# Attention phase: feed-forward products through one PSUM bank, the double banks for scores alone

## The chip, the cores and the metric

The kernel runs on one core of one Trainium2 chip. Its time is device microseconds from start to end of the program. The profile's busy times, waits and orders come from one profiled execution. TensorE does matmuls and transposes into PSUM (eight banks of 512 fp32 columns a partition), ScalarE exponentials and other functions, VectorE and GpSimd elementwise work, SyncE issues DMAs. The engines run side by side, each in its own order, and wait for each other by semaphores.

## The reference

Two layers; the change is in the attention phase of the first. It computes causal attention of 8 heads with two maps each over 4 x 1024 tokens of 128 channels, and, independent of it, the feed-forward gate of the same tokens, with its inputs rounded blockwise to a 4-bit grid:

```python
scores = jnp.einsum('bhqd,bhkd->bhqk', q, k)
scores = jnp.where(causal[None, None], scores, -jnp.inf)
attn = jax.nn.softmax(scores.astype(jnp.float32), axis=-1).astype(scores.dtype)
...
out = jnp.einsum('bhqk,bhkd->bhqd', attn, v)
...
gate = fp4_linear(x, w_gate)     # rounds x and w in blocks of 16, then a product
y = fp4_linear(x, w_up)
h = jax.nn.silu(gate) * y
return fp4_linear(h, w_down)     # rounds h too
```

## The kernel before

`attention_phase` works in `ITER` = 8 iterations: the first and the last written out, six in a loop on every engine. An iteration handles two slots (a slot is four score maps, each of 8 head dimensions in a row group of 32) and four feed-forward tiles of 128 tokens (`GT` = 4).

A slot is ten units (`NU`), listed by `chunk_units`: a unit is 512 columns of queries against one block of 128 keys. Blocks on the diagonal have fewer columns; units 1 and 8 join 384 and 128 columns ("in two pieces"), units 2 and 9 have 256 columns ("narrow"). For each unit TensorE makes scores in two pairs of maps (`scores`, L933): a pair fills a double bank of a ring of three (`ring`), one bank for each of its maps. ScalarE turns a pair into probabilities (`exp`, L787). GpSimd masks diagonal blocks (`mask`, L731). Three units later TensorE multiplies by the values into `ps_o` (`values`, L953). VectorE turns `ps_o` (L839) and divides.

A feed-forward tile goes: gate product (`gate`, L961), ScalarE's tanh (L801), VectorE's first product (L846), up product (`up`, L965), VectorE's second product (L851), seven steps that round the hidden rows (`fp4_part`), three transposes (`turn_hidden`, L972), VectorE's copies (L861, L862), down product (`down`, L978), tanh (L806), VectorE's product (L865). Once an iteration x is rounded for the next in seven such steps (`round_x`), turned (`turn_x`, L918) and copied (L843).

No scheduler sets the order. Each engine's `place(it, n)` is called for ticks n = 0 to 79 (four a unit), and for what is left of the iteration before at n + 80; in it each piece of work stands at a fixed tick. What an engine issues is the order of those calls, and semaphores alone set the time. The ring is dealt out by a list of its uses in order:

```python
GATE, HIDDEN, DOWN, CHUNK = 3, 7, 9, 11
ORDER = [("x", 0)]
for k in range(STEPS):
    if k % PERIOD == GATE:
        ORDER.append(("gate", k // PERIOD))
    ORDER += [("scores", k, 0), ("scores", k, 1)]
```

So 45 uses an iteration: 40 for scores, four for gate and up products, which share a double bank until VectorE's second product, and one for the turned x. `wait_free` makes TensorE wait until the third use before is finished. `ps_f`, a single bank, holds the turned hidden rows and the down product.

## Time and profile before

| what | value |
| --- | --- |
| three runs | 751.53, 753.23, 757.88 us; median 753.23 |
| the profiled execution | 757.34 us, of which the span is 755.6 |
| busy in the span: TensorE | 609.4 us (81%) |
| VectorE | 531.1 us (70%) |
| ScalarE | 497.5 us (66%) |
| GpSimd | 323.8 us (43%) |
| ScalarE's exponentials (L787) | 320, 280.1 us busy |
| values (L953) | 1536 matmuls, 158.3 us busy |
| scores (L933) | 672 matmuls in the loop and after, 80.1 us busy |

The span runs from the first to the last instruction. The attention phase is the stretch from 115.2 us to about 454 us. An engine's busy time counts the time in which at least one of its instructions runs; instructions that follow each other on ScalarE, VectorE and TensorE overlap by a part of their duration, so starts tell more than durations. A row of the order of time reads: start, duration, engine, line, output and input, number of instructions merged, and in brackets how long the engine was idle before and whose result ended that.

### The profile page before, as it was taken

To read this page: it belongs to the slowest core of one execution; us is meant where nothing else is said; L and a number is where in the kernel's file an instruction comes from. 1 tells how busy PE (TensorE), PEld (TensorE's weight loads), DVE (VectorE), ACT (ScalarE), POOL (GpSimd) and SP (SyncE) were. 2 spreads that over 40 slices of the span, in tenths; PEclk is the share of its full clock that TensorE was granted. 3 is DMA by queue.
4 is the path that set the end of the run, shared out by engine and by line. 5 is a ranking of instruction groups with operands and counts; after the bars stand their busy time and mean duration, and the time that the engine had idled before them with its cause. 6 is when DMAs were issued, how large, how long until landed. Compare 5 with 4: busy or idle time off the path is not lost. (4 is left out here: it accounts for less than half of the span.)

```text
span 755.6 us, 15892 instructions
## 1 busy us (share of the span) xinstructions
PE 609.4 (81%) x4825; PEld 365.0 (48%) x4826; DVE 531.1 (70%) x1428; ACT 497.5 (66%) x843; POOL 323.8 (43%) x463
## 2 busy tenths in 40 slices
PE   4567666999999999999999997866873787888970
PEld 3455451333333333333333346655762686777860
DVE  3999996879798888888897777964734342434475
ACT  2277875989898999989898971432423454656561
POOL 0243354444343444344444435154645355554551
PEclk9899996999999999999999998996977799999995
DMA  7000001004555555666566005111112122222285
GB/s 198 15 28 23 19 1 56 1 2 87 97 91 97 85 87 89 105 105 105 105 105 106 3 1 196 35 38 55 55 50 57 47 75 64 65 79 66 77 244 149
DMA packets 76264, 56.05 MB, mean 74 GB/s; under 512 B 6528, under 2 KB 70848, under 8 KB 75968
## 3 DMA queue, kind: packets, MB, share of 16 engines
q1 hardware_dynamic: 70688, 46.01, 29.1%
q0 software_dynamic: 4352, 8.99, 3.5%
q10 hardware_dynamic: 1184, 0.56, 0.3%
q8 instruction: 20, 0.33, 0.2%
q14 instruction: 20, 0.16, 0.1%
HBM read 15.36 MB, written 28.65 MB: 58 GB/s over the span
## 5 line engine op out<-in xcount | busy, mean ns | idle before, releaser
L787 ACT ACTIVATE attend_prob<-attend_ring 128x1024 f32<-128x1024 f32 (+1 forms) x320 | 280.1, 951 | 17.5 <-PE attend_ring L933 15.5
L731 POOL TENSOR_SCALAR_AFFINE_SELECT attend_prob<-attend_prob 128x256 f32<-128x256 f32 x256 | 118.6, 488 | 142.4 <-ACT attend_prob L787 141.1
L953 PE MATMUL attend_ps_o<-attend_prob,attend_v_slot 128*32 128x512 f32 (+3 forms) x1536 | 158.3, 501 | 0.0
L1906 POOL DMA_INDIRECT expert_outputs<-routed_linear_gated,routed_expert_goal_now x72 | 70.9, 985 | 69.3 <-DVE routed_linear_gated L1950 55.0
L1033 POOL DMA_INDIRECT slots<-rows,slot_index x64 | 61.7, 964 | 67.5 <-issue 37.2
L933 PE MATMUL attend_ring<-attend_qk_slot 32*128 32x512 f16 (+3 forms) x672 | 80.1, 329 | 8.1 <-ACT attend_prob L787 6.3
L933 PEld LDWEIGHTS attend_ring<-attend_qk_slot 32*128 32x128 f16 x672 | 22.4, 91 | 106.7 <-ACT attend_prob L787 37.6
L1927 DVE TENSOR_TENSOR outed_linear_head_normed<-outed_linear_head_normed,routed_linear_ps_c 128x256 f32<-128x256 f32 x72 | 30.2, 420 | 50.1 <-ACT outed_linear_head_normed L2020 31.0
L2067 PE MATMUL routed_linear_ps_c<-outed_linear_head_normed,head_turned 128*128 128x128 f32 x384 | 54.5, 288 | 6.1 <-ACT outed_linear_head_normed L1996 5.0
L2020 ACT ACTIVATE outed_linear_head_normed<-routed_linear_ps_c 128x256 f32<-128x256 f32 x72 | 27.5, 382 | 47.2 <-PE routed_linear_ps_c L2067 36.1
L953 PEld LDWEIGHTS attend_ps_o<-attend_prob,attend_v_slot 128*32 128x32 f32 x1536 | 33.9, 109 | 45.8 <-issue 38.3
L2067 PEld LDWEIGHTS routed_linear_ps_c<-outed_linear_head_normed,head_turned 128*128 128x128 f32 x384 | 49.7, 202 | 7.0 <-ACT outed_linear_head_normed L1996 4.6
L369 POOL TENSOR_TENSOR project_parts_q<-project_rotated_q,project_parts_q 128x1024 f16<-128x1024 f32 x8 | 17.6, 2202 | 68.8 <-ACT project_parts_q L417 68.8
L839 DVE STREAM_TRANSPOSE attend_o_t<-attend_ps_o 128x512 f32<-128x512 f32 x32 | 22.9, 717 | 18.3 <-PE attend_ps_o L953 18.3
L2001 ACT ACTIVATE head_turned<-w 128x512 f32 x48 | 30.4, 634 | 4.4 <-issue 4.4
L1542 ACT ACTIVATE routed_linear_qk_square<-routed_linear_ps_c 128x512 f32<-128x512 f32 x16 | 9.5, 592 | 36.1 <-PE routed_linear_ps_c L1650 19.9
L1650 PE MATMUL routed_linear_ps_c<-att_w,routed_linear_xn_turned 128*128 128x384 f32 x64 | 29.2, 588 | 4.7 <-DVE routed_linear_qk L1248 4.7
L978 PEld LDWEIGHTS attend_ps_f<-down_w,attend_hq_t 128*128 128x128 f32 (+1 forms) x192 | 23.8, 190 | 17.8 <-issue 16.4
L2076 PE MATMUL routed_linear_ps_f<-w,outed_linear_head_normed 128*128 x144 | 24.2, 292 | 9.7 <-DVE outed_linear_head_normed L1927 5.6
L978 PE MATMUL attend_ps_f<-down_w,attend_hq_t 128*128 128x128 f32 (+1 forms) x192 | 29.9, 292 | 1.1 <-DVE attend_hq_t L862 1.1
L394 ACT ACTIVATE qk_parts<-project_ps_turn 128x1024 f16 (+1 forms) x30 | 29.0, 1021 | 2.6 <-PE project_ps_turn L475 2.6
L2076 PE MATMUL routed_linear_ps_b<-w,outed_linear_head_normed 128*128 x144 | 24.1, 292 | 7.3 <-DVE routed_linear_gated L1950 5.8
(290 smaller groups left out, 1285.7 us busy)
## 6 DMA issues: line engine op xcount, KB each, us to landing
slots<-attend_zeros SPq DMA_DIRECT2D x24, 715.0 KB, 10.3
attend_qk_slot<-qk_parts SPq DMA_DIRECT2D x14, 512.0 KB, 3.1
x_pairs<-slots SPq DMA_DIRECT2D x72, 65.0 KB
v_all<-expert_outputs SPq DMA_DIRECT2D x8, 512.0 KB
xn_all<-project_xn SPq DMA_DIRECT2D x8, 256.0 KB, 2.3
w<-w_laid SPq DMA_DIRECT2D x1, 2048.0 KB, 7.8
rows<-rows SPq DMA_DIRECT2D x4, 512.0 KB
out<-xn_all SPq DMA_DIRECT2D x8, 256.0 KB, 3.7
```

The costliest lines, as they stand in the source:

```text
L731: ins = nc.gpsimd.affine_select(out=edge, in_=edge, compare_op=ALU.is_ge, fill=0.0, base=0, pattern=[[0, 2], [1, P]], channel_multiplier=-1)
L787: nc.scalar.activation(probs(k, pair)[:, :, 0:width], scores[:, :, 0:width], ACT.Exp, scale=HD ** -0.5).then_inc(exp_made[u][pair], 1)
L933: ins = nc.tensor.matmul(dst[:, s * QC + at:s * QC + at + cols], qk[rows, T + j * P:T + (j + 1) * P], qk[rows, qc * QC + off:(qc + 1) * QC ...
L953: ins = nc.tensor.matmul(ps_o[RB * s:RB * (s + 1), off:QC], v4[slot][:, j, s], probs(k, s // 2)[:, s % 2, at:at + cols], start=j == 0, sto ...
L978: ins = nc.tensor.matmul(ps_f[:, 0:P], hq_t[0:r, c * P:(c + 1) * P], m.down_w[0:r, c * P:(c + 1) * P], start=c == 0, stop=c == 2)
L1033: pool.indirect_dma_start(m.slots, bass.IndirectOffsetOnAxis(m.slot_index[u][c][:, j:j + 1], 0), m.rows[c][:, t * ROW:(t + 1) * ROW], None ...
L1650: ins = nc.tensor.matmul(bank_pair(part)[:, j, 0:3 * C], xt[:, tile * P:(tile + 1) * P], m.att_w[:, 4 * P:7 * P], start=True, stop=True)
L1906: pool.indirect_dma_start(m.outputs, bass.IndirectOffsetOnAxis(goal_now[i][:, j:j + 1], 0), y_out[i][:, j * P:(j + 1) * P], None).then_inc ...
L1927: nc.vector.tensor_tensor(act_e[c], silu[c], ps_h[c][:, EI:2 * EI], ALU.mult).then_inc(a_made, 1)
L2001: nc.scalar.activation(w_now[s % 3], m.w13[:, ds(expert * (2 * EI), 2 * EI)], ACT.Copy).then_inc(w_kept, 1)
L2067: ins = nc.tensor.matmul(ps_h[s % 3][:, f * P:(f + 1) * P], w_now[s % 3][:, f * P:(f + 1) * P], x_t[s % 3], start=True, stop=True)
L2076: ins = nc.tensor.matmul(ps_y[s % 2][:, 0:P], act_e[s % 3][:, c * P:(c + 1) * P], m.w2[:, ds(expert * EI + c * P, P)], start=c == 0, stop= ...
```

## The change

Seven things, all in `attention_phase`:

- Gate and up products, the turned x, the turned hidden rows and the down product all go through `ps_f`, one after the other. The gate product waits until an earlier tile's down product is read, the up product until VectorE's first product has read the gate (`u_made`), the hidden transposes until its second has read the up product (`h_made`).
- The ring is used by scores alone, 36 times an iteration.
- A narrow unit's two pairs share one double bank, side by side in its columns. [...] One exponential of 1024 columns takes the place of two of 512, one mask of four blocks the place of two.
- The unit before a narrow one issues its first pair at its own step and its second at the narrow unit's.
- Tiles start at ticks 0, 20, 40 and 60 (in the first iteration at 12, 28, 44 and 60). Counted from a tile's start, the gate product stands at tick 1, up at 5, the transposes of the tile before at 9 and its down product at 13. x is turned at tick 77.
- VectorE's steps stand at other ticks; x's rounding is at 18, 19, 38, 39, 58, 58 and 59.
- The end of the last iteration follows these places.

The core of the diff:

```diff
-        GATE, HIDDEN, DOWN, CHUNK = 3, 7, 9, 11
-        PERIOD = STEPS // GT
-        ORDER = [("x", 0)]
+        GATE, UP, HIDDEN, DOWN = 1, 5, 9, 13
+        FIRST_TURN, NEXT_TURN, CHUNK = 9, TICKS - 3, 46
+        ORDER = []
         for k in range(STEPS):
-            if k % PERIOD == GATE:
-                ORDER.append(("gate", k // PERIOD))
-            ORDER += [("scores", k, 0), ("scores", k, 1)]
+            ORDER += [("scores", k, pair) for pair in range(1 if k % NU in NARROW else 2)]
...
+                if u in NARROW:
+                    nc.scalar.activation(prob[2 * k % PROBS], buffer("scores", k, 0), ACT.Exp, scale=HD ** -0.5).then_inc(exp_made[u][0], 1)
+                    return
...
+                for part, tick in enumerate((18, 19, 38, 39, 58, 58, 59)):
...
-                wait_free(it, "scores", k, pair)
-                dst = buffer("scores", k, pair)
+                if u in NARROW and pair == 1:
+                    pe.wait_ge(first_pair_made[u], 2 * it + slot + 1)
+                else:
+                    wait_free(it, "scores", k, pair)
+                dst = buffer("scores", k, 0 if u in NARROW else pair)
                 for j, off, at, cols in segs:
+                    at += pair * HALF if u in NARROW else 0
...
             def gate(it, i):
                 pe.wait_ge(xt_kept, it + 1)
-                wait_free(it, "gate", i)
-                nc.tensor.matmul(buffer("gate", i)[:, 0:INNER], xq_t[:, i * P:(i + 1) * P], m.gu_w[:, 0:INNER], start=True,
+                if i == 1 and isinstance(it, int) and it == 0:
+                    pe.wait_ge(h_made, 1)
+                elif i >= 1:
+                    pe.wait_ge(g_made, 4 * it + i - 1)
+                nc.tensor.matmul(ps_f[:, 0:INNER], xq_t[:, i * P:(i + 1) * P], m.gu_w[:, 0:INNER], start=True,
                                  stop=True).then_inc(gate_made, 1)
 
             def up(it, i):
-                nc.tensor.matmul(buffer("gate", i)[:, QC:QC + INNER], xq_t[:, i * P:(i + 1) * P], m.gu_w[:, INNER:2 * INNER],
+                pe.wait_ge(u_made, 4 * it + i + 1)
+                nc.tensor.matmul(ps_f[:, 0:INNER], xq_t[:, i * P:(i + 1) * P], m.gu_w[:, INNER:2 * INNER],
                                  start=True, stop=True).then_inc(up_made, 1)
 
             def turn_hidden(it, i):
                 pe.wait_ge(hq_made, 4 * it + i + 1)
-                once(pe, g_made, 4 * it + i)
+                if isinstance(it, int) and it == ITER - 1 and i == GT - 1:
+                    pe.wait_ge(g_made, 4 * it + i)
+                else:
+                    pe.wait_ge(h_made, 4 * it + i + 2)
...
             def place(it, n):
                 k, tick = divmod(n, 4)
...
+                if k < STEPS and tick == 0:
+                    if k % NU in NARROW:
+                        scores(it, k - 1, 1)
+                    scores(it, k, 0)
+                    if (k + 1) % NU not in NARROW:
+                        scores(it, k, 1)
...
+                if n == NEXT_TURN and not (isinstance(it, int) and it == ITER - 1):
+                    turn_x(it + 1)
+                if (i := at_tile(it, n, GATE)) is not None:
+                    gate(it, i)
+                if (i := at_tile(it, n, UP)) is not None:
+                    up(it, i)
+                if (i := behind_tile(it, n, HIDDEN)) is not None:
+                    turn_hidden(it, i)
+                if (i := behind_tile(it, n, DOWN)) is not None:
+                    down(it, i)
                 if tick == 2 and 0 <= k - LAG < STEPS:
                     values(it, k - LAG)
```

TensorE in the loop, around the first slot's second tile, before (L972 transposes, L961 gate, L965 up, L933 scores, L953 values):

```order
L953 MATMUL attend_ps_o<-attend_prob,attend_v_slot 32x512 x4
L972 MATMUL attend_ps_f<-ident,attend_hq 128x128 x2
L972 MATMUL attend_ps_f<-ident,attend_hq 96x128
L961 MATMUL attend_ring<-gate_up_w,attend_xq_t 128x352
L933 MATMUL attend_ring<-attend_qk_slot 128x384 x2
L933 MATMUL attend_ring<-attend_qk_slot 128x128 x2
L965 MATMUL attend_ring<-gate_up_w,attend_xq_t 128x352
L933 MATMUL attend_ring<-attend_qk_slot 128x384 x2
L933 MATMUL attend_ring<-attend_qk_slot 128x128 x2
L953 MATMUL attend_ps_o<-attend_prob,attend_v_slot 32x512 x4
```

And now (L996 gate, L1001 up, L1011 transposes, L962 scores, L985 values):

```order
L962 MATMUL attend_ring<-attend_qk_slot 128x512 x4
L996 MATMUL attend_ps_f<-gate_up_w,attend_xq_t 128x352
L985 MATMUL attend_ps_o<-attend_prob,attend_v_slot 32x256 x4
L962 MATMUL attend_ring<-attend_qk_slot 128x512 x4
L1000 REGISTER_ALU
L1001 MATMUL attend_ps_f<-gate_up_w,attend_xq_t 128x352
L985 MATMUL attend_ps_o<-attend_prob,attend_v_slot 32x512 x4
L962 MATMUL attend_ring<-attend_qk_slot 128x512 x4
L1011 MATMUL attend_ps_f<-ident,attend_hq 128x128 x2
L1011 MATMUL attend_ps_f<-ident,attend_hq 96x128
L985 MATMUL attend_ps_o<-attend_prob,attend_v_slot 32x512 x4
```

The gate product stands alone between scores and values, one step before the up product, the transposes of the tile before come a step later, and no pair of scores stands behind the up product.

TensorE in the loop, at units 1 and 2 of the first slot, before:

```order
L933 MATMUL attend_ring<-attend_qk_slot 128x384 x2
L933 MATMUL attend_ring<-attend_qk_slot 128x128 x2
L86 ISA
L933 MATMUL attend_ring<-attend_qk_slot 128x384 x2
L933 MATMUL attend_ring<-attend_qk_slot 128x128 x2
L953 MATMUL attend_ps_o<-attend_prob,attend_v_slot 32x384 x4
L953 MATMUL attend_ps_o<-attend_prob,attend_v_slot 32x128 x4
L933 MATMUL attend_ring<-attend_qk_slot 128x256 x4
L953 MATMUL attend_ps_o<-attend_prob,attend_v_slot 32x256 x4
```

And now:

```order
L1001 MATMUL attend_ps_f<-gate_up_w,attend_xq_t 128x352
L985 MATMUL attend_ps_o<-attend_prob,attend_v_slot 32x384 x4
L985 MATMUL attend_ps_o<-attend_prob,attend_v_slot 32x128 x4
L86 ISA
L962 MATMUL attend_ring<-attend_qk_slot 128x384 x2
L962 MATMUL attend_ring<-attend_qk_slot 128x128 x2
L962 MATMUL attend_ring<-attend_qk_slot 128x256 x4
L1005 ISA
L1009 REGISTER_ALU
L1011 MATMUL attend_ps_f<-ident,attend_hq 128x128 x2
L1011 MATMUL attend_ps_f<-ident,attend_hq 96x128
L985 MATMUL attend_ps_o<-attend_prob,attend_v_slot 32x256 x4
```

Unit 1's second pair has moved behind the values of one step, next to unit 2's four matmuls of 256 columns; the up product and the transposes stand in the gaps.

VectorE in the loop, between the third tile's rounding and the fourth tile's products, before (L573, L576 of `attend_xq`: x's steps; L882: the sum of head squares; L846, L851: the two products):

```order
L821 TENSOR_TENSOR attend_o_scaled<-attend_o_t,attend_rden 128x256
L573 SCALAR_TENSOR_TENSOR attend_xq_power<-attend_xq 128x512
L576 SCALAR_TENSOR_TENSOR attend_xq<-attend_xq_power,attend_xq 128x512
L882 ISA
L882 TENSOR_REDUCE head_var<-attend_head_square 128x32
L839 STREAM_TRANSPOSE attend_o_t<-attend_ps_o 128x512
L861 COPY attend_hq_t<-attend_ps_f 128x256
L862 COPY attend_hq_t<-attend_ps_f 96x128
L845 REGISTER_ALU
L846 SCALAR_TENSOR_TENSOR attend_hidden<-attend_gate_tanh,attend_ring 128x352
L851 TENSOR_TENSOR attend_hidden<-attend_hidden,attend_ring 128x352
```

And now (L578 to L583 of `attend_xq`: x's steps; L916; L871, L876):

```order
L892 SCALAR_TENSOR_TENSOR xn_all<-attend_down_tanh,attend_ps_f 128x128
L581 SCALAR_TENSOR_TENSOR attend_hq<-attend_hq_power,attend_hq 128x352
L583 TENSOR_TENSOR attend_hq<-attend_hq,attend_hq_scale 128x352
L578 SCALAR_TENSOR_TENSOR attend_xq<-attend_xq_power,attend_xq 128x512
L581 SCALAR_TENSOR_TENSOR attend_xq<-attend_xq_power,attend_xq 128x512
L583 TENSOR_TENSOR attend_xq<-attend_xq,attend_xq_scale 128x512
L916 ISA
L916 TENSOR_REDUCE head_var<-attend_head_square 128x32
L870 REGISTER_ALU
L871 SCALAR_TENSOR_TENSOR attend_hidden<-attend_gate_tanh,attend_ps_f 128x352
```

Three of x's steps and the sum of squares stand in one row directly ahead of the tile's first product (L871).

## Rows read from the trace of the kernel before

**Rows 1.** Windows: us of each engine, one iteration of the loop, then the first iteration
```profile
core 0: us, PE busy (x) PEld busy (x) DVE busy (x) ACT busy (x) POOL busy (x), PEclk, DMA share, GB/s
...
161.90:202.45 40.55, 39.39 (x348) 14.28 (x344) 33.92 (x76) 37.07 (x48) 17.38 (x35) 1.00 0.32 60
...
115.20:161.90 46.70, 41.15 (x311) 14.01 (x311) 34.11 (x72) 36.96 (x47) 20.80 (x40) 0.85 0.06 23
```

**Rows 2.** One line: L843, VectorE copies x's turned rows, once an iteration
```profile
L843 DVE COPY attend_xq_t<-attend_ring x7: 692/692/692, 161.9 to 405.2; 128x512 f32<-128x512 f32 x7
```

**Rows 3.** Order of time: TensorE's matmuls (start us, duration us)
```profile
203.63 0.58 PE L933 MATMUL attend_ring<-attend_qk_slot 32*128 32x384 f16 x8
...
204.13 1.07 PE L953 MATMUL attend_ps_o<-attend_prob,attend_v_slot 128*32 128x384 f32 x16
...
205.65 0.28 PE L933 MATMUL attend_ring<-attend_qk_slot 32*128 32x256 f16 x2 [0.23 <-ACT attend_prob L787]
...
205.86 0.64 PE L953 MATMUL attend_ps_o<-attend_prob,attend_v_slot 128*32 128x256 f32 x8
...
206.43 0.55 PE L972 MATMUL attend_ps_f<-ident,attend_hq 128*128 128x128 f32 x3
...
206.81 0.76 PE L961 MATMUL attend_ring<-gate_up_w,attend_xq_t 128*128 128x352 f32 x2
...
207.50 0.39 PE L933 MATMUL attend_ring<-attend_qk_slot 32*128 32x512 f16 x2
...
207.82 0.86 PE L965 MATMUL attend_ring<-gate_up_w,attend_xq_t 128*128 128x352 f32 x2
...
208.61 0.39 PE L933 MATMUL attend_ring<-attend_qk_slot 32*128 32x512 f16 x2
...
208.93 1.06 PE L953 MATMUL attend_ps_o<-attend_prob,attend_v_slot 128*32 128x512 f32 x8
...
209.93 0.40 PE L933 MATMUL attend_ring<-attend_qk_slot 32*128 32x512 f16 x4
...
211.25 0.94 PE L978 MATMUL attend_ps_f<-down_w,attend_hq_t 128*128 128x128 f32 x6
...
212.12 0.40 PE L933 MATMUL attend_ring<-attend_qk_slot 32*128 32x512 f16 x4
...
212.44 0.64 PE L953 MATMUL attend_ps_o<-attend_prob,attend_v_slot 128*32 128x256 f32 x8
...
213.02 0.39 PE L933 MATMUL attend_ring<-attend_qk_slot 32*128 32x512 f16 x2
...
213.63 0.39 PE L933 MATMUL attend_ring<-attend_qk_slot 32*128 32x512 f16 x2 [0.22 <-ACT attend_prob L787]
```

**Rows 4.** Order of time: ScalarE, the same stretch
```profile
207.60 0.47 ACT L801 ACTIVATE attend_gate_tanh<-attend_ring 128x352 f32<-128x352 f32 x1
...
210.35 1.94 ACT L787 ACTIVATE attend_prob<-attend_ring 128x1024 f32<-128x1024 f32 x2 [0.29 <-PE attend_ring L933]
...
212.55 5.60 ACT L787 ACTIVATE attend_prob<-attend_ring 128x1024 f32<-128x1024 f32 x6
...
217.99 0.52 ACT L801 ACTIVATE attend_gate_tanh<-attend_ring 128x352 f32<-128x352 f32 x1
...
218.34 2.08 ACT L787 ACTIVATE attend_prob<-attend_ring 128x1024 f32<-128x1024 f32 x2
...
220.60 1.09 ACT L787 ACTIVATE attend_prob<-attend_ring 128x512 f32<-128x512 f32 x2 [0.19 <-PE attend_ring L933]
...
222.46 0.28 ACT L806 ACTIVATE attend_down_tanh<-attend_ps_f 128x128 f32<-128x128 f32 x1 [0.78 <-PE attend_ps_f L978]
```

**Rows 5.** VectorE: one step in order of time, then groups by line
```profile
208.78 0.52 DVE L851 TENSOR_TENSOR attend_hidden<-attend_hidden,attend_ring 128x352 f32<-128x352 f32 x1 [0.16 <-PE attend_ring L965]
...
L576 DVE SCALAR_TENSOR_TENSOR attend_xq<-attend_xq_power,attend_xq 128x512 f32<-128x512 f32 x6 | 4.7, 776 | 0.2
...
L882 DVE TENSOR_REDUCE head_var<-attend_head_square 128x512 f32 x6 | 4.0, 674 | 0.0
```

**Rows 6.** Order of time: ScalarE in the first iteration
```profile
124.30 0.46 ACT L801 ACTIVATE attend_gate_tanh<-attend_ring 128x352 f32<-128x352 f32 x1 [3.91 <-PE attend_ring L961]
```

More of the change, by code:

```diff
@@ L552 @@
 LAST = [max(u for u, unit in enumerate(UNITS) if unit[0] == qc) for qc in range(NQC)]
+HALF = QC // 2
+NARROW = [u for u, (_, segs) in enumerate(UNITS) if sum(seg[3] for seg in segs) == HALF]
 FP4_PARTS = 7
@@ L602, in attention_phase @@
         TICKS = 4 * STEPS
[L603 removed]
+        LATE = TICKS + 59
         FIRST_REC = TICKS + 12
@@ L663, in probs, with starts, at_tile, behind_tile @@
         def probs(k, pair):
+            if k % NU in NARROW:
+                return prob[2 * k % PROBS].rearrange("p (s w c) -> p w s c", w=2, c=HALF)[:, pair]
             return prob[(2 * k + pair) % PROBS].rearrange("p (s c) -> p s c", c=QC)
-        def at_tile(n, step, tick):
-            i, rest = divmod(n - 4 * step - tick, 4 * PERIOD)
-            return i if rest == 0 and 0 <= i < GT else None
+        PERIOD = TICKS // GT
+        def starts(it):
+            if isinstance(it, int) and it == 0:
+                return [12, 28, 44, 60]
+            return [i * PERIOD for i in range(GT)]
+        def at_tile(it, n, tick):
+            return next((i for i, s in enumerate(starts(it)) if n == s + tick), None)
+        def behind_tile(it, n, tick):
+            return next((i for i, s in enumerate(starts(it)[1:] + [TICKS]) if n == s + tick), None)
         def run(eng, place):
@@ L863, in place @@
[L863 to L867 removed]
+                c, rest = divmod(n - CHUNK, PERIOD)
+                if rest == 0 and 0 <= c < 2 * NQC:
@@ L868, in place @@
                     divide_o(it, c // NQC, c % NQC)
-                for part, (step, tick) in enumerate(((6, 3), (7, 0), (8, 0), (11, 3), (12, 0), (16, 3), (18, 0))):
-                    if n == 4 * step + tick and not (isinstance(it, int) and it == ITER - 1):
+                for part, tick in enumerate((18, 19, 38, 39, 58, 58, 59)):
+                    if n == tick and not (isinstance(it, int) and it == ITER - 1):
                         if part == 2:
```

140 lines of the change are left out of this document (67 added, 73 removed).

## The prediction

> **What bounds the kernel now.** [...] Eight iterations fill the stretch from 115.2 to about 445.8 us: one of 46.7 us, in part at a lower clock (mean 0.85), and seven of 40.55. So the question is which engine is late in an iteration, and the order of time answers it [rows 3, 4]. The reader should take starts, not durations: the next instruction's start shows what each costs its engine.
>
> TensorE, start to start [rows 3]: scores of a full unit, both pairs, 0.32 us (212.12 to 212.44, where the values behind them start; the same for one pair, 208.61 to 208.93); values of a wide unit 1.00 (208.93 to 209.93; I take the same for a unit in two pieces, whose columns are as many); of a narrow one 0.58 (212.44 to 213.02); three transposes of the hidden rows 0.38 with the gate product behind them; that gate product 0.69; the up product 0.79, since it comes behind scores; the down product 0.87; scores of a unit in two pieces 0.50 for both pairs, of a narrow unit 0.21 (205.65 to 205.86, one pair; I take both alike). For half an iteration (ten units, two feed-forward tiles) that makes: values 8 x 1.00 + 2 x 0.58 = 9.16; scores 5 x 0.32 + 0.50 + 2 x 0.21 + 2 x 0.64 (the two units whose pairs the up product parts) = 3.80; feed-forward 2 x (0.38 + 0.69 + 0.79 + 0.87) = 5.46. Sum 18.4 of the 20.27 that half an iteration lasts: TensorE waits under 2 us.
>
> ScalarE [rows 4]: six exponentials of 1024 from 212.55 to the tanh at 217.99, 0.91 each; of 512, 0.50 (1.09 for two, less the last one's 0.59); the tanh of a gate 0.35. It waits 0.29 before 210.35, because the scores wait until a gate's buffer of the ring is free, and 0.78 before the down product's tanh at 222.46. Neither engine is the bound alone: they hold each other through the ring of three buffers.
>
> **The change, part by part.**
>
> Exponentials of narrow units: four times an iteration two of 512 (1.00) become one of 1024 (0.91): ScalarE gains 0.4 us an iteration, on an engine that waits for TensorE anyway; I count nothing. GpSimd's masks there become one of 512 columns for four selects; GpSimd is busy 17.38 of 40.55 us [rows 1]: nothing.
>
> Scores: the up product no longer parts two pairs. The two units go from 0.64 to 0.32: minus 0.64. The units before the narrow ones are now parted instead, the first pair alone at 0.32. At the narrow unit TensorE issues the other pair (0.18, what the divided unit's 0.50 is above 0.32), the narrow unit's first pair, and its second, which now waits until the first has landed. No row shows TensorE waiting for itself. The nearest is how long scores take to reach another engine, 209.93 to 210.35 [rows 3, 4], 0.42 for 512 columns; with half the columns 0.11 less (that is what narrow scores are below wide ones, 0.21 and 0.32), so 0.31, and 0.02 to start again: 0.33. The bounds are 0.11, the columns alone, and 0.42; I take 0.33, since landing and release are the same thing in both. Then 0.21 as before: 0.72 for the step. Scores come to 6 x 0.32 + 2 x 0.32 + 2 x 0.72 = 4.00, plus 0.20 a half.
>
> Feed-forward: the gate product stood behind the transposes and now stands between scores and values, where the up product's price holds, 0.79 instead of 0.69 [rows 3]. The transposes lose their neighbour and get the cost of passing to another shape, 0.48. Sum 2 x (0.79 + 0.79 + 0.48 + 0.87) = 5.86, plus 0.40. TensorE's list is thus 9.16 + 4.00 + 5.86 = 19.0, plus 0.6 a half.
>
> [...]
>
> The ring: 36 uses instead of 45 an iteration, all by scores. The wait for the hidden product (0.29 on ScalarE) goes. What is late next is found by following the loop of dependences. Count from the start of the exponential of unit 4's first pair. 1.08 later (212.55 to 213.63, [rows 3, 4]) TensorE may issue unit 5's second pair; 0.32 on, the gate product; 0.90 on (206.81 to 207.60, plus the 0.10) ScalarE's tanh starts, at 2.30, though ScalarE was free at 1.82: a wait of 0.48 that the new place of the product makes. 0.35 on, unit 5's first exponential; 1.08 on, at 3.73, unit 6's second pair, for which TensorE has waited since 2.77 (1.40 + 0.79 + 0.58). From there it never waits until unit 14: 2.11 (scores, up, values) + 1.80 (scores, transposes, values) + 2.19 (with down) + 1.72 (narrow step, values) + 2.11 + 2.11 + 1.78 (narrow step, transposes, narrow values) + 2.19 = 16.0. Then 0.42 to unit 14's exponential, which is where the count began. The loop is 3.73 + 16.0 + 0.42 = 20.15 us.
>
> x's turning: four transposes behind three of 0.48, so 0.6, once an iteration on this path. x's rounding: its last three steps and the sum of squares now stand in a row ahead of the fourth tile's first product on VectorE: 0.78 + 0.67 + 0.67 + 0.67 (the first step and the sum have rows, the two between are taken as long as the sum) [rows 5]. Following VectorE's list from the third tile, that product ends at about 4.2 on the scale above, and the up product's place on TensorE is at 4.05: 0.2 us of wait, behind which the values and scores are queued. Elsewhere the product ends at 3.35, or 0.1 before its up product.
>
> So an iteration takes 2 x 20.15 + 0.6 + 0.2 = 41.1 instead of 40.55: plus 0.55, seven times, plus 3.9. In the first iteration scores no longer queue behind the gate product for which ScalarE waits 3.91 us [rows 6], but the four tiles are packed into 64 ticks where TensorE is the slower one, and its last steps have none: 0 within 1 us either way, a judgement. The end gains about as much as one order of transposes and values, within 0.5. Sum plus 3.8. On the profiled execution (757.34 us, span 755.6 and 1.7 around it) that gives 761.1; the three runs' median is 753.23, so **757.0 us**.
>
> **The rivals.**
>
> A, the double banks pay (faster). If the gate product's tanh doesn't hold ScalarE, or if the first pair's landing costs 0.11, its waits of 1.1 a half (20.15 less 19.0) vanish and TensorE's list alone sets the pace: 2 x 19.0 + 0.6 = 38.6, minus 1.95 an iteration, minus 14 us: 739. For it: TensorE has waits to give, and the ring's gate uses are gone. Against: the tanh's input comes 0.48 us after ScalarE is free in both tiles of a half, by rows. Chance 0.18, with all that comes out below 745.7.
>
> B, VectorE becomes the bound (slower). One bank now carries gate, up, transposes and down in turn, so TensorE stands at the up product until VectorE's first product has read the gate. By the above the margin there is 0.1 us in every other tile. If x's steps, or masks that GpSimd writes beside VectorE's, hold VectorE 0.3 us longer than counted, that is 0.3 us in three tiles of four, 0.9 an iteration, 7 more us: 764. It decides once that product is over 0.1 us later than counted. For it: VectorE is at 84% [rows 1] and already waits only 0.16 us for an up product [rows 5]. Chance 0.30, with all above 760.8.
>
> C, the parts cancel: within 1% of before (about what a measurement of this kernel can tell from no change), the forecast among them: 0.52. TensorE's list grows by 0.6 a half; its waits, 1.9 a half before (20.27 less 18.4, x's turning among them), come to 1.5 (1.1, and 0.4 for x's turning and VectorE). A difference of two sums of small terms is easily off by its own size.
>
> D, the change does not do what it says: the same waits come back under other names and only ScalarE's saving counts, minus 0.4 us an iteration: 750. It is inside C.
>
> **How the numbers follow.** Forecast 757.0. Of the unknown costs the pair's landing (0.11 to 0.42, four times) moves an iteration by minus 0.9 to plus 0.4, so minus 7 to plus 3 us; the price of a lone product, 0.05 us off at 16 places, plus or minus 6; VectorE's order 0 to plus 7. Taken together with A reached most of the way, the range is 742 to 769, which leaves out about one in ten at either end. Faster by over 1% 0.18, within 1% 0.52, slower by over 1% 0.30.
>
> **What would show it.** Right: copies of x's turned rows 41.0 to 41.2 us apart; TensorE busy for nearly all of it; ScalarE idle before each gate's tanh by some 0.5 us, waiting for TensorE, and no longer before scores behind a gate; the second pair of a narrow unit starting 0.3 us after the first; the gate product 0.79 long, start to start. Wrong: a distance under 40 us (A), where the tanh follows the exponential without a gap; or long waits of the up product for VectorE, or of VectorE's product behind x's steps (B). The forecast fails by its sign if the loop through the gate's tanh is not the one that closes, since then those 1.1 us of TensorE's waits are not there.

## The result, and the profile of the changed kernel

The changed kernel takes 763.63 us (median of 4 runs, 762.2 to 766.24), the kernel before 755.04 (median of 4 on the same chip, 751.53 to 757.88): a ratio of 1.0134, 95% interval 1.0079 to 1.0189. So it is slower by 1.3%, some 10 us (6 to 14), where the forecast had plus 3.8 us. (The two medians are 8.6 us apart, inside that interval.)

Medians and spans are a coarse measure here, the distance between two copies of x's turned rows a fine one: behind the first iterations it repeats to 0.02 us within a run, but for the last distance of the kernel before (40.46) and one iteration of one run below. First the line that copies them, VectorE in the changed kernel; it answers to [rows 2]:

```profile
L862 DVE COPY attend_xq_t<-attend_ps_f x8: 692/693/694, 123.6 to 413.5; 128x512 f32<-128x512 f32 x8
```

The first of the eight belongs to the first iteration. From the third on (206.11 to 413.53, five steps) they are 41.48 us apart; before it was 40.55. The page's groups say which engine waits for which (line, operation, count, busy us, mean ns, then idle us before them and what ended it):

```profile
L811 ACT ACTIVATE attend_prob<-attend_ring 128x1024 f32<-128x1024 f32 x256 | 247.8, 1035 | 24.9 <-PE attend_ring L962 24.6
...
L962 PE MATMUL attend_ring<-attend_qk_slot 32*128 32x512 f16 (+3 forms) x672 | 70.6, 329 | 11.1 <-ACT attend_prob L811 8.1
...
L825 ACT ACTIVATE attend_gate_tanh<-attend_ps_f 128x352 f32<-128x352 f32 x32 | 14.9, 464 | 25.2 <-PE attend_ps_f L996 25.2
...
L1001 PE MATMUL attend_ps_f<-gate_up_w,attend_xq_t 128*128 128x352 f32 x64 | 28.2, 522 | 3.4 <-DVE attend_hidden L871 3.4
```

ScalarE waits 25.2 us for gate products; TensorE waits 8.1 for exponentials and 3.4 for VectorE at the up product. Both can be seen at the fourth tile of an iteration, TensorE in order of time (start, duration; in brackets idle time and who ended it):

```profile
236.72 0.39 PE L962 MATMUL attend_ring<-attend_qk_slot 32*128 32x512 f16 x2
237.03 0.86 PE L996 MATMUL attend_ps_f<-gate_up_w,attend_xq_t 128*128 128x352 f32 x2
237.82 0.64 PE L985 MATMUL attend_ps_o<-attend_prob,attend_v_slot 128*32 128x256 f32 x8
238.39 0.39 PE L962 MATMUL attend_ring<-attend_qk_slot 32*128 32x512 f16 x2
239.36 0.39 PE L962 MATMUL attend_ring<-attend_qk_slot 32*128 32x512 f16 x2 [0.58 <-ACT attend_prob L811]
240.32 0.86 PE L1001 MATMUL attend_ps_f<-gate_up_w,attend_xq_t 128*128 128x352 f32 x2 [0.57 <-DVE attend_hidden L871]
```

The gate product (L996) costs 0.79, start to start; then unit 6's second pair stands until 239.36, because its buffer is freed by the exponential behind the gate's tanh; ScalarE at the same place:

```profile
235.64 1.94 ACT L811 ACTIVATE attend_prob<-attend_ring 128x1024 f32<-128x1024 f32 x2
237.93 0.46 ACT L825 ACTIVATE attend_gate_tanh<-attend_ps_f 128x352 f32<-128x352 f32 x1 [0.35 <-PE attend_ps_f L996]
238.29 1.93 ACT L811 ACTIVATE attend_prob<-attend_ring 128x1024 f32<-128x1024 f32 x2
```

The up product then stands 0.64 longer than its 0.32, since VectorE reaches the first product of the tile (L871) only at 239.76, behind three steps of x's rounding and the heads' sum:

```profile
237.11 0.68 DVE L578 SCALAR_TENSOR_TENSOR attend_xq<-attend_xq_power,attend_xq 128x512 f32<-128x512 f32 x1
237.83 0.69 DVE L581 SCALAR_TENSOR_TENSOR attend_xq<-attend_xq_power,attend_xq 128x512 f32<-128x512 f32 x1
238.55 0.69 DVE L583 TENSOR_TENSOR attend_xq<-attend_xq,attend_xq_scale 128x512 f32<-128x512 f32 x1
239.16 0.68 DVE L916 TENSOR_REDUCE head_var<-attend_head_square 128x512 f32 x1
239.76 0.51 DVE L871 SCALAR_TENSOR_TENSOR attend_hidden<-attend_gate_tanh,attend_ps_f 128x352 f32<-128x352 f32 x1
```

**Where the time went.** All by the starts of exponentials, in the two profiled executions:

| stretch | before | after | difference |
|---|---|---|---|
| first exponential | 115.63 | 117.28 | +1.65 (the same code until there) |
| first iteration, its first exponential to the next one's | 46.55 | 49.74 | +3.19 |
| six iterations of the loop | 6 x 40.55 | 6 x 41.48 | +5.58 |
| last iteration, to its last exponential | 38.42 | 38.31 | -0.11 |
| from there to the next stage | 11.89 | 10.70 | -1.19 |
| from there to the end of the span | 299.8 | 295.5 | -4.3 (the same code) |

The attention stage lost 7.5 us (3.19 + 5.58 - 0.11 - 1.19). The last row is no gain: over the fourteen profiled kernels of this study, all with that code, the stretch is 295.5 to 301.4 us. That is why the two spans differ by only 4.8 us.

### The profile page after: what moved, and what is told of

Its sections match the earlier page's. It is cut to its first block and busy times, and to the rows that moved or that the text cites. A ratio compares the mean times of both kernels' runs of the same rounds, so it can differ in the third digit from the quotient of the medians.

```text
span 760.4 us, 15777 instructions
## 1 busy us (share of the span) xinstructions
PE 611.9 (80%) x4825; PEld 365.8 (48%) x4826; DVE 538.6 (71%) x1428; ACT 491.0 (65%) x811; POOL 323.5 (43%) x431
## 5 line engine op out<-in xcount | busy, mean ns | idle before, releaser
L811 ACT ACTIVATE attend_prob<-attend_ring 128x1024 f32<-128x1024 f32 x256 | 247.8, 1035 | 24.9 <-PE attend_ring L962 24.6
L985 PE MATMUL attend_ps_o<-attend_prob,attend_v_slot 128*32 128x512 f32 (+3 forms) x1536 | 158.4, 500 | 0.2
L752 POOL TENSOR_SCALAR_AFFINE_SELECT attend_prob<-attend_prob 128x256 f32<-128x256 f32 x192 | 88.7, 479 | 160.2 <-ACT attend_prob L811 160.2
L962 PE MATMUL attend_ring<-attend_qk_slot 32*128 32x512 f16 (+3 forms) x672 | 70.6, 329 | 11.1 <-ACT attend_prob L811 8.1
L962 PEld LDWEIGHTS attend_ring<-attend_qk_slot 32*128 32x128 f16 x672 | 19.8, 91 | 111.8 <-issue 87.5
L985 PEld LDWEIGHTS attend_ps_o<-attend_prob,attend_v_slot 128*32 128x32 f32 x1536 | 33.7, 108 | 61.8 <-issue 52.9
L871 DVE SCALAR_TENSOR_TENSOR attend_hidden<-attend_gate_tanh,attend_ps_f 128x352 f32<-128x352 f32 x32 | 16.3, 508 | 25.4 <-ACT attend_gate_tanh L825 25.4
L807 ACT ACTIVATE attend_prob<-attend_ring 128x1024 f32<-128x1024 f32 x32 | 32.6, 1020 | 0.0
L825 ACT ACTIVATE attend_gate_tanh<-attend_ps_f 128x352 f32<-128x352 f32 x32 | 14.9, 464 | 25.2 <-PE attend_ps_f L996 25.2
L1001 PE MATMUL attend_ps_f<-gate_up_w,attend_xq_t 128*128 128x352 f32 x64 | 28.2, 522 | 3.4 <-DVE attend_hidden L871 3.4
```

The costliest lines, as they stand in the source:

```text
L752: ins = nc.gpsimd.affine_select(out=edge, in_=edge, compare_op=ALU.is_ge, fill=0.0, base=0, pattern=[[0, 2], [1, P]], channel_multiplier=-1)
L807: nc.scalar.activation(prob[2 * k % PROBS], buffer("scores", k, 0), ACT.Exp, scale=HD ** -0.5).then_inc(exp_made[u][0], 1)
L811: nc.scalar.activation(probs(k, pair)[:, :, 0:width], scores[:, :, 0:width], ACT.Exp, scale=HD ** -0.5).then_inc(exp_made[u][pair], 1)
L962: ins = nc.tensor.matmul(dst[:, s * QC + at:s * QC + at + cols], qk[rows, T + j * P:T + (j + 1) * P], qk[rows, qc * QC + off:(qc + 1) * QC ...
L985: ins = nc.tensor.matmul(ps_o[RB * s:RB * (s + 1), off:QC], v4[slot][:, j, s], probs(k, s // 2)[:, s % 2, at:at + cols], start=j == 0, sto ...
```

## The experiments

Twelve kernels, each an edit of the changed one. The table has the loop's iteration and the first iteration, both by the trace, and of the first iteration the time that TensorE ran at the lower granted clock (0.50 of full speed). The last column is the ratio of times to the kernel before on the same chip where a kernel was executed several times, and otherwise the time of its one execution, which says little, as executions of one kernel lie up to 12 us apart.

| run | iteration, us | first iteration, us | of it at clock 0.50, us | ratio to before, 95%, or one time |
|---|---|---|---|---|
| before | 40.55 | 46.55 | 13.7 | 1 |
| the change | 41.48 | 49.74 | 13.7 | 1.0134 (1.0079 to 1.0189) |
| x's rounding early | 40.84 | 50.52 | 17.1 | 1.0113 (1.0022 to 1.0203) |
| gate product first | 41.22 | 48.04 | 10.2 | 1.0101 (1.0017 to 1.0185) |
| second pair behind transposes | 41.13 | 47.06 | 6.8 | 1.0100 (1.0015 to 1.0186) |
| first iteration spread | 41.48 | 49.12 | 13.7 | 1.0164 (1.0075 to 1.0253) |
| the first three together | 40.03 | 48.60 | 13.5 | 1.0007 (0.9967 to 1.0047) |
| those, first iteration's x moved | 40.03 | 45.10 | 10.2 | 0.9932 (0.9899 to 0.9966) |
| first iteration's x moved, alone | 41.49 | 46.39 | 10.2 | 762.57 us |
| masks cut | 41.30 | 47.97 | 10.2 | 760.38 us |
| two exponentials again | 41.48 | 48.03 | 10.2 | 763.81 us |
| tanh behind an exponential | 41.54 | (46.86) | 10.2 | 766.18 us |
| 0.9932's kernel without the pair's move | 40.31 | 45.88 | 10.2 | 750.98 us |
| 0.9932's kernel with the tanh behind | 41.77 | (43.67) | 6.8 | 1.0106 (1.0066 to 1.0146) |

The two first iterations in parentheses can't be set beside the others: there the second iteration's first exponential, which ends the stretch, stands ahead of the tanh. By the first two copies of x's turned rows the run with the tanh behind has 39.20 us, the one with the gate product first 39.23 and the changed kernel 40.92.

**x's rounding early.**

```diff
-                for part, tick in enumerate((18, 19, 38, 39, 58, 58, 59)):
+                for part, tick in enumerate((0, 1, 18, 19, 38, 39, 39)):
```

> All seven steps of x's rounding stand before tick 40 (0, 1, 18, 19, 38, 39, 39), where VectorE has gaps; ahead of the fourth tile's gate product only the reduction of the heads' squares is left. Theory 'VectorE at the fourth tile': the up product's wait there (0.96 us from scores (6,1) to the up product, 0.32 elsewhere) goes, and the distance between two turnings of x falls by 0.64 from 41.48 to 40.85, 7 times, so some 4.5 us in all. Rival 'the wait is hidden by the dependences that follow': the up product comes 0.64 sooner and TensorE waits as much longer for the next exponential, 41.4 to 41.5, no change in time.

Measured 40.84. The up product of the fourth tile, TensorE in this run:

```profile
239.41 0.39 PE L962 MATMUL attend_ring<-attend_qk_slot 32*128 32x512 f16 x2 [0.58 <-ACT attend_prob L811]
239.72 0.86 PE L1001 MATMUL attend_ps_f<-gate_up_w,attend_xq_t 128*128 128x352 f32 x2
```

It comes 0.31 behind the scores, without a wait: the 0.64 is VectorE's, and nothing behind takes it back. Of the 3.8 us that six iterations gain, little is in the time: the first iteration got longer, as its third gate product waits 1.84 us for VectorE (1.25 in the changed kernel) and 6.8 us at the lower clock (0.50) follow.

**Gate product first.** In TensorE's `place`, for tiles two to four from the second iteration on, the gate product is issued ahead of the scores of its step.

```diff
+                first = isinstance(it, int) and it == 0
+                if not first and (i := at_tile(it, n, 0)):
+                    gate(it, i)
...
-                if (i := at_tile(it, n, GATE)) is not None:
+                if (i := at_tile(it, n, GATE)) is not None and (first or i == 0):
```

> From the second iteration on the gate products of tiles two to four are issued ahead of the scores of their step, not behind them; VectorE's x steps stay where the change put them. Theory 'dependences through the gate's tanh': the gate's tanh starts 0.35 to 0.47 sooner (0.50 us of scores no longer ahead of the gate; ScalarE's exponentials end 0.35 before the tanh starts now), TensorE's wait ahead of the second pair of unit 6 falls from 0.97 to 0.5-0.6 at tiles two and four, and the half iteration from 20.13 to 19.7; in the half with x the up product's wait for VectorE stays or grows by up to 0.4. Iteration 40.7 to 41.1. Rival 'TensorE's own list sets the pace': the list is no shorter, so 41.4 to 41.5 an iteration.

Measured 41.22, a little above the range expected. From the second tile's tanh to the fourth's it is 19.68 us where the changed kernel has 20.12: the 0.44 is there. In the other half it goes to the wait for VectorE:

```profile
236.02 0.39 PE L962 MATMUL attend_ring<-attend_qk_slot 32*128 32x512 f16 x2
236.70 0.39 PE L962 MATMUL attend_ring<-attend_qk_slot 32*128 32x512 f16 x2 [0.30 <-ACT attend_prob L811]
238.12 0.86 PE L1001 MATMUL attend_ps_f<-gate_up_w,attend_xq_t 128*128 128x352 f32 x2 [1.03 <-DVE attend_hidden L871]
```

The wait for the exponential shrinks from 0.58 to 0.30, the one for VectorE grows from 0.57 to 1.03.

**Second pair behind the transposes.** In three of the four narrow units.

```diff
-                    if (k + 1) % NU not in NARROW:
+                    if (k + 1) % NU not in NARROW and k not in (2, 12, 19):
                         scores(it, k, 1)
...
+                if tick == 1 and k in (2, 12, 19):
+                    scores(it, k, 1)
```

> The second pair of three of the four narrow units is issued behind the transposes that follow it, so that it need not stand 0.325 us waiting for the first pair to land. Theory 'the landing costs TensorE 0.15 each (0.325 less the 0.173 that the issue takes) and its list is part of the dependences through the tanh': 0.15 times 3, iteration 41.0 instead of 41.48, 3 us in all. Rival 'the landing wait has cover, since TensorE waits for exponentials anyway': the wait for the exponential ahead of unit 6's second pair grows from 0.97 to 1.1 and nothing is gained.

Measured 41.13, so 0.35 of the 0.46 that the landing was thought to cost at three places. The 0.325 of the expectation is the distance from the last matmuls started ahead of the second pair (the unit before's 128 columns, 211.31) to the pair (211.63); from the narrow unit's first pair (211.15), which the trace has beside the unit before's, it is 0.48. Here the transposes stand between (227.47) and the pair takes 0.22 (227.94 to 228.16):

```profile
227.47 0.55 PE L1011 MATMUL attend_ps_f<-ident,attend_hq 128*128 128x128 f32 x3
227.94 0.28 PE L962 MATMUL attend_ring<-attend_qk_slot 32*128 32x256 f16 x2
228.16 0.64 PE L985 MATMUL attend_ps_o<-attend_prob,attend_v_slot 128*32 128x256 f32 x8
```

**First iteration spread.**

```diff
-                return [12, 28, 44, 60]
+                return [12, 29, 46, 62]
```

> Only the first iteration's tiles start at ticks 12, 29, 46, 62 instead of 12, 28, 44, 60, so that a tile's last product has 1 to 2 ticks more before the next gate product needs the bank. Theory 'the close packing of four tiles costs the 3.2 us of the first iteration': the waits of 1.3 and 1.0 us of TensorE ahead of gate products three and four shrink by 0.5 each and the time falls by about 1 us. Rival 'the first iteration lost its 3 us to TensorE's half-speed stretches and VectorE's load there': less than 0.3 us changes in the first iteration. Later iterations stay at 41.48 in both.

0.6 us shorter in the trace (49.12), with as much of the lower clock as the changed kernel (13.7 us), and so between the two theories' 1 us and 0.3. The third gate product's wait of 1.25 is gone, but the fourth's is 1.14 instead of 0.91, and the turning of x behind it waits 1.31 us for the same step of VectorE. The ratios can't tell 0.6 us.

**The first three together.**

> The edits of the three earlier runs together: x's rounding before tick 40, the gate products of tiles two to four ahead of their step's scores, the narrow units' second pair behind the transposes. With x's rounding early, VectorE takes the fourth gate product at once, so the gate that is issued sooner is worth its 0.44 us in both halves. Theory 'three separate lengths of one loop': 41.48 less 0.64, less 2 times 0.44, less 0.35, gives 39.6 an iteration, 0.95 under the kernel before, and a time 1 to 7 us under it if the first iteration stays 2 to 3 us longer. Rival 'they share one slack': what one edit frees, the next cannot free again, and the iteration stays at 40.5 or more, no faster than before.

Measured 40.03 and a time equal to before. Of 0.64, 0.88 and 0.35 expected, 1.45 us of 1.87 came. With the run without the pair's move (40.31, below) it splits into 0.64 for x's rounding, 0.53 for the gate products beside it and 0.28 for the pair: the gate products are short of 0.88. One piece that is missing can be placed: from the second tile's tanh to the third's it is 10.35 us where the gate-first run alone has 10.15, since three steps of x now stand ahead of the third tile and the last step of the tile before is late. The gate product shows it, waiting for VectorE:

```profile
213.68 0.83 PE L996 MATMUL attend_ps_f<-gate_up_w,attend_xq_t 128*128 128x352 f32 x2 [0.17 <-DVE xn_all L892]
```

**The same, with the first iteration's x steps at ticks of their own.**

```diff
-                for part, tick in enumerate((0, 1, 18, 19, 38, 39, 39)):
+                for part, tick in enumerate((12, 13, 15, 16, 17, 31, 64) if isinstance(it, int) and it == 0 else (0, 1, 18, 19, 38, 39, 39)):
```

> The same, and in the first iteration alone x's rounding stands at ticks 12, 13, 15, 16, 17, 31, 64, where VectorE waited for the tanh and the up product of tiles one, two and four. Theory 'VectorE's load holds up the first iteration's gate products': TensorE's waits ahead of gate products three and four (1.3 and 1.0 us in the changed kernel) fall under 0.6 each, the clock does not fall to half in that iteration, and from the first exponential to the second turning of x is 1 to 3 us less than in the run without it. Rival 'the packing itself, 16 ticks a tile, leaves too little between the down product's tanh and the next gate': the waits stay above 1 us and nothing changes. Later iterations as in the run without it.

3.5 us less in the first iteration, 40.03 in the others, and 0.9932 of the kernel before (0.9899 to 0.9966): the only version whose interval lies under 1. Of the 3.5 us, 1.9 come between the second and the third tanh (10.47 to 8.59) and 0.5 ahead of the first (9.12 to 8.66). The other 1.2 (9.60 to 8.43, first to second tanh) are the clock's: x's place makes no difference there (8.44 in the run with x's rounding early), but the lower clock lasts 4.4 us of that stretch in the one kernel and 1.8 in the other.

**The first iteration's x steps alone, on the changed kernel.**

> The changed kernel with only the first iteration's x steps moved to ticks 12, 13, 15, 16, 17, 31, 64. Same two theories as for the run with all edits: waits ahead of gate products three and four under 0.6 us each and some 1.5 us less in the first iteration, or unchanged. Later iterations 41.48.

46.39 instead of 49.74. The waits of the third and fourth gate products, first in the changed kernel:

```profile
143.61 0.83 PE L996 MATMUL attend_ps_f<-gate_up_w,attend_xq_t 128*128 128x352 f32 x2 [1.25 <-DVE xn_all L892]
...
153.15 0.83 PE L996 MATMUL attend_ps_f<-gate_up_w,attend_xq_t 128*128 128x352 f32 x2 [0.91 <-DVE xn_all L892]
```

and in this run:

```profile
140.89 0.86 PE L996 MATMUL attend_ps_f<-gate_up_w,attend_xq_t 128*128 128x352 f32 x2
...
149.48 0.86 PE L996 MATMUL attend_ps_f<-gate_up_w,attend_xq_t 128*128 128x352 f32 x2
```

They waited for VectorE's last step of the tile before, and with x's rounding elsewhere they don't. From the second tanh to the fourth it is 17.18 us for 19.42, so 2.24 of the 3.35 us is x's place, and the packing into 16 ticks does not by itself bring these waits. The rest is the clock: 1.6 behind the fourth tanh, where this run has no fall (last section), less 0.5 between the first two, where it ran longer at the lower clock (3.3 us at 0.50, against 2.3).

**Masks cut.** GpSimd's selects cover one element instead of 128 columns a head; the upper part of the diagonal blocks stays in.

> The changed kernel with GpSimd's masks cut to one element each, so that the upper part of the diagonal blocks is left in. Theory 'GpSimd's masks slow VectorE beside them': the rounding steps of the hidden tile that took 0.84 and 1.25 us at the first tile of an iteration take 0.53 to 0.55, as others do; the fourth tile's gate product comes sooner and the up product's wait of 0.64 us falls by 0.1 to 0.4. Rival 'the long steps are due to something else': they stay at 0.8 and more. The iteration falls by what the up product's wait does, to 41.1 to 41.4; not at all if VectorE's end ahead of the fourth tile does not move.

Measured 41.30; the up product's wait fell by 0.18 (0.57 to 0.39 in brackets). Of the two rounding steps one lost its long cases, the other kept them, as the lines show. The changed kernel (shortest, median, longest, ns):

```profile
L575 DVE SCALAR_TENSOR_TENSOR attend_hq_power<-attend_hq x32: 524/614/842, 132.2 to 450.9; 128x352 f32<-128x352 f32 x32
...
L578 DVE SCALAR_TENSOR_TENSOR attend_hq<-attend_hq_power,attend_hq x32: 524/704/1248, 132.8 to 451.5; 128x352 f32<-128x352 f32 x32
```

Masks cut, the same lines:

```profile
L575 DVE SCALAR_TENSOR_TENSOR attend_hq_power<-attend_hq x32: 524/526/1400, 130.3 to 446.8; 128x352 f32<-128x352 f32 x32
...
L578 DVE SCALAR_TENSOR_TENSOR attend_hq<-attend_hq_power,attend_hq x32: 524/526/541, 130.9 to 447.4; 128x352 f32<-128x352 f32 x32
```

In this run the medians of both lines are 526 ns, so masks explain the middle; the long case moved with GpSimd's scaling of the values, which the cut masks let start earlier (211.02 here, beside L575 at 211.04 and its 1.40 us; 214.62 in the changed kernel, beside L578 at 215.06 and its 1.25). The expectation named only the masks; by these rows both of GpSimd's jobs do it, though no run takes the other one away.

It matters ahead of the fourth tile's product, where VectorE works without a gap from the copies at 232.56 on. There GpSimd stages the other slot's values, by a copy (L733). The changed kernel:

```profile
234.31 0.84 DVE L575 SCALAR_TENSOR_TENSOR attend_hq_power<-attend_hq 128x352 f32<-128x352 f32 x1
234.73 0.89 POOL L733 COPY attend_v_slot<-v_all 128x512 f32 x1
235.19 0.81 DVE L578 SCALAR_TENSOR_TENSOR attend_hq<-attend_hq_power,attend_hq 128x352 f32<-128x352 f32 x1
```

Masks cut:

```profile
231.13 0.60 POOL L733 COPY attend_v_slot<-v_all 128x512 f32 x1
231.17 0.95 DVE L575 SCALAR_TENSOR_TENSOR attend_hq_power<-attend_hq 128x352 f32<-128x352 f32 x1
232.15 0.52 DVE L578 SCALAR_TENSOR_TENSOR attend_hq<-attend_hq_power,attend_hq 128x352 f32<-128x352 f32 x1
```

The two steps take 1.65 us and 1.47, which is the 0.18; of the 1.47, 0.43 is above twice 0.52, in the step beside the copy.

**Two exponentials again** in each narrow unit, on the changed kernel.

```diff
-                    nc.scalar.activation(prob[2 * k % PROBS], buffer("scores", k, 0), ACT.Exp, scale=HD ** -0.5).then_inc(exp_made[u][0], 1)
+                    both = buffer("scores", k, 0).rearrange("p (s w c) -> p w s c", w=2, c=HALF)
+                    for half in range(2):
+                        ins = nc.scalar.activation(probs(k, half), both[:, half], ACT.Exp, scale=HD ** -0.5)
+                    ins.then_inc(exp_made[u][0], 1)
```

> The changed kernel with the one exponential of a narrow unit (1.02 us for 1024 columns) split into two of 512 again (0.61 us each in the kernel before). It undoes the one part of the change that takes work from an engine: ScalarE gets 0.1 to 0.2 us more a narrow unit, 0.4 to 0.8 an iteration. Theory 'TensorE and the tanh's turn set the time, the joined exponential is worth little': 41.5 to 41.7 an iteration, since ScalarE waits 2.4 us an iteration for gate products and 3 for scores. Rival 'ScalarE's list counts in full': 41.9 to 42.3.

41.48 to 0.01: what the change takes from ScalarE is worth nothing in the loop.

**The gate's tanh behind the first exponential** of its step, from the second iteration on, on the changed kernel (ScalarE's `place`: the tanh at tick `GATE`, after `exp`).

> The changed kernel with the gate's tanh behind the first exponential of its step instead of ahead of it (from the second iteration on). The exponential of scores (5,0) no longer waits for the gate, so TensorE's 0.65 us beyond the issue ahead of the second pair of unit 6 goes; the tanh starts some 0.45 later (218.25 for 217.80), so the up product takes over 0.4 of it. Theory 'the tanh stands in the loop of dependences': half without x 19.9 instead of 20.13, iteration 41.0 to 41.3, with the up product's wait for VectorE at the fourth tile as before. Rival 'whatever is freed is waited for at the up product in full': 41.4 to 41.5.

41.54: the rival was right. Unit 6's second pair waits no more, but the up product starts 1.06 us behind it instead of 0.32 (second tile), as it needs the tanh and VectorE's product. The tanh ahead of the exponential was not the loop by itself.

**The 0.9932 kernel without the second pair's move.**

> The kernel with four edits (x's rounding early, in the first iteration at ticks of its own; gate products first; narrow units' second pair behind the transposes) without the last one. Alone that edit was worth 0.35 us an iteration. With the gate products first the half without x came to 19.71 with it and 19.68 without it. Theory 'beside the other edits the landing of the first pair is covered by the wait for exponentials': 40.0 to 40.1 an iteration in this run too. Rival 'it is worth 0.35 still, in the half with x': 40.3 to 40.4.

40.31, so that edit is worth 0.28 beside the others as well (0.35 alone): the rival was right and the landing has little cover. My expectation had compared halves of two kernels that differed in x's place too.

**All edits and the tanh behind.**

> All edits together, with the gate's tanh behind the first exponential of its step as well. In the kernel with the other edits ScalarE issues from one exponential to the next without a gap around the tanh, yet TensorE waits 0.33 to 0.43 us beyond the issue ahead of unit 6's second pair, for the exponential behind the tanh. Theory 'the tanh's place ahead of that exponential is what is left of the loop': 39.6 to 39.8 an iteration instead of 40.03, 2 to 3 us less in all, and some 0.990 of the kernel before. Rival 'the up product then waits for the tanh instead': 40.0 or more.

41.77 and 1.0106: 1.74 us an iteration worse than without it, so the rival was right by more than it said. The up product waits for VectorE at three of the four tiles (0.6 to 0.8 us beyond the scores' issue), and the wait that was to go is still there:

```profile
213.26 0.39 PE L966 MATMUL attend_ring<-attend_qk_slot 32*128 32x512 f16 x2 [0.22 <-ACT attend_prob L811]
214.17 0.86 PE L1005 MATMUL attend_ps_f<-gate_up_w,attend_xq_t 128*128 128x352 f32 x2 [0.52 <-DVE attend_hidden L875]
```

## Why the prediction was right in kind and short in size

**The sign and the loop: right.** The half iteration without x was forecast at 20.15 us, counted along gate product, tanh, exponential, unit 6's second pair and TensorE's list. The trace has 20.13 (exponentials behind the tanh at 218.16 and 238.29). The terms hold one by one: gate and up product 0.79, the down product 0.87, transposes 0.48, and 0.71 for a narrow unit's step of scores (231.26 to 231.97) for the 0.72 that was built on a landing of 0.33. (The sign named for it, a second pair 0.3 us after the first, holds from the last matmuls ahead of it, 0.325; from the first pair itself it is 0.48.) The 0.02 "to start again" in that 0.33 is my estimate, which no run shows apart, and every run keeps the second pair's wait, so none shows whether the pair needs it. ScalarE's wait ahead of the tanh was to be 0.48 and is 0.47 by starts. The gate product takes 0.79 behind scores (237.03 to 237.82), where it took 0.69 behind the transposes in the kernel before; what the 0.10 consists of, no run shows. The runs confirm the loop from its side: issuing the gate 0.5 us sooner took 0.44 from a half, and moving the landing behind other work took 0.28 to 0.35 from an iteration. Rival A (TensorE's list alone, 38.6) is out: even with three edits the iteration is 40.03. Rival D, that ScalarE's saving counts 0.4, is out by the run with two exponentials, as the forecast's "I count nothing" had it.

**The step that was mis-sized: "0.2 us of wait" for VectorE at the fourth tile.** It measures 0.64 by starts, and x's rounding moved away takes exactly 0.64 from the iteration. That half came to 21.35 for 20.95 forecast, and 41.48 for 41.1 an iteration is this one term. The count put VectorE's product at 4.2 and the up product's place at 4.05; the second was right (3.73 + 0.32), but the up product starts at 4.68 (240.32, counted from 235.64). The row that the forecast names as the reason was priced right: x's three steps and the sum take 2.65 us (237.11 to 239.76) for the 2.79 counted. Late is what stands ahead of it, the hidden rows' steps, for which the forecast shows no price: two of them take 0.84 and 0.81 where they take 0.52 alone, 0.61 too much together. Cutting the masks gives back 0.18 of it, which is shown; the rest stands beside GpSimd's copy of the values, by the rows alone. Rival B had named this mechanism, masks included, but in three tiles of four at 0.3; it came in one, at 0.64.

**The first iteration: "0 within 1 us" was 3.19.** The judgement looked at the packing of the tiles. The place was VectorE again: the same x steps held up the last step of a tile, on which the next gate product waits for the bank, by 1.25 and 0.91 us. Moved, 2.24 us go from these two places. The clock does not explain the difference to the kernel before: both ran 13.7 us of that iteration at 0.50, the kernel before all at its start, the changed one 10.2 at its start and 3.4 in a fall near the end that cost it 1.6 (last section). What the start's low clock cost the kernel before can't be told from its one trace, so some 1 us of the 3.19 is not placed.

**The rest.** The forecast took seven longer iterations; the seventh, the last, turns no x and is 0.1 shorter, and the end gained 1.2 for the 0.5 allowed. With 5.6 in the loop and 3.2 in front, 7.5 us stands against the 3.8 of the sum; the measured 10 us has an interval that begins at 6.

**What was luck.** The time lies in the range, but in the class that had a chance of 0.30 (slower by over 1%; the interval reaches under 1%), and the sign named for being right, copies 41.0 to 41.2 apart, was missed with 41.48. That it falls on rival B's 764 is luck: B added 0.9 an iteration for waits at three tiles of four. The loop is 0.4 above the forecast, for one tile, and the rest came in the first iteration, for which B had nothing.

**The unconfirmed part.** That the tanh's place ahead of the exponential made the loop was only half right: the loop closes through the up product just as well, as the two runs with the tanh behind show.

## What to carry to other kernels

When several products share one bank, every reader of the bank is in TensorE's path (here VectorE, for 0.64 us at one up product and 1.25 and 0.91 at two gate products): place an engine's spare work (here x's rounding) by what waits behind it, not by whether the engine has a gap on average. Count a loop of dependences from start to start; that gave 20.15 for 20.13. And test edits together as well as alone: the early gate product gained 0.26 an iteration alone and 0.53 where x's rounding was out of its way (40.84 to 40.31).

## What the hardware showed

**VectorE beside GpSimd.** A rounding step with two inputs takes 0.52 us alone, and up to 1.25 beside GpSimd's scaling of the values (1.40 in the masks-cut run). VectorE's reduction of the same tile, with one input, has a median of 520 ns in both kernels, and never more than 521 in the changed one, though GpSimd works beside 23 of its 32. Why the one gets longer and the other does not, no run shows.

**The clock.** Every first iteration has the granted clock at 0.50 near its start, from 2.5 us behind its first exponential at the latest, for 6.8 to 13.7 us from one kernel's trace to the next, and from the first to the second tanh the changed kernel and its edits take 8.15 us with 0.6 us of that stretch at the lower clock, 8.65 with 2.3 and 9.60 with 4.4. So first iterations can be compared only with this beside them (the table's fourth column). The granted clock also fell in the middle of dense work. In the changed kernel's first iteration:

```profile
150.00:155.00 5.00, 3.96 (x38) 1.79 (x38) 4.86 (x11) 3.02 (x5) 0.00 (x0) 1.00 0.00 0
155.00:160.00 5.00, 4.55 (x23) 1.24 (x26) 2.73 (x8) 3.57 (x5) 0.00 (x0) 0.66 0.00 0
```

The run with the gate product first has the same code there, the same waits, and no fall:

```profile
150.00:155.00 5.00, 3.88 (x38) 1.71 (x38) 4.86 (x11) 3.03 (x5) 0.00 (x0) 1.00 0.00 0
155.00:160.00 5.00, 4.63 (x34) 1.62 (x35) 4.23 (x11) 5.00 (x7) 0.56 (x1) 1.00 0.00 0
```

The first iteration is 49.74 us with the fall (to 0.50 for 3.4 us) and 48.04 without: 1.7 us, of which 1.6 stand behind the fourth tanh. The runs with x's rounding early, the first iteration spread and the masks cut have such a fall in that iteration too. It came once inside the loop as well, in the run with the tanh behind, in the one iteration that took 43.12 instead of 41.54, while TensorE stood 1.39 us at an up product:

```profile
360.00:365.00 5.00, 3.61 (x20) 0.98 (x22) 4.49 (x9) 4.26 (x6) 0.00 (x0) 0.81 0.00 1
```

Each of these falls followed waits of 0.9 to 1.8 us on TensorE, and the same waits came in other runs and iterations without one; whether a wait has a part in it stays open. Where the changed kernel had the fall, it cost 1.6 us.
